# Channel attention: queries and keys projected once, and laid into the score strips through a strip image in DRAM

## What is computed

```python
q = jnp.einsum('oc,bct->bot', Wq, target) + bq[None, :, None]      # target: normalised x, 128 x 256 per batch
k = jnp.einsum('oc,bcs->bos', Wk, source) + bk[None, :, None]      # source: context
v = jnp.einsum('oc,bcs->bos', Wv, source) + bv[None, :, None]
# 16 heads of 8 rows each
dot = jnp.einsum('bhdt,bhds->bhts', q, k) / math.sqrt(HEAD_DIM)
mask = target_mask[:, :, :, None] * source_mask[:, :, None, :]
dot = mask * dot - (1.0 - mask) * NEG
amap = jax.nn.softmax(dot, axis=-1) * mask
out = jnp.einsum('bhts,bhds->bhdt', amap, v)
```

## Time and profile before

| | |
|---|---|
| median of 3 runs | 1764.23 us (1762.54 to 1769.84) |
| profiled execution | 1761.46 us, span of its trace 1759.6 us |
| mean granted clock | 0.984 |
| busy, share of the span | PE 95%, DVE 65%, ACT 56%, POOL 33% |
| channel attention | until about 310 us |
| a batch of it in the middle | 15.05 us |

### The profile page before, as it was taken

One profiled execution on the slowest core, in us unless ns is written; L12 is line 12 of the kernel. 1 busy time (PEld: TensorE's weight loads), 2 busy tenths in 40 slices (PEclk: granted clock), 3 DMA queues, 4 the chain that ended last, 5 costly groups with the idle time before them and its releaser, 6 DMA issues. The chain is left out here.

```text
span 1759.6 us, 34328 instructions
## 1 busy us (share of the span) xinstructions
PE 1676.9 (95%) x11824; PEld 1419.5 (81%) x11832; DVE 1139.4 (65%) x2540; ACT 992.1 (56%) x2502; POOL 584.2 (33%) x638
## 2 busy tenths in 40 slices
PE   7999997798999999999999999999999998899997
PEld 6666664368788988889898989888898997689985
DVE  6888888897556656656566655555555567954434
ACT  2788875686545555545556555545545543555553
POOL 4444426435511111112122111111111212877774
PEclk9999997899999999999999999999999999999999
DMA  6011122102100100100100011001000004443448
GB/s 209 14 31 32 32 81 96 60 1 101 52 13 13 45 5 14 49 1 13 37 25 25 13 65 37 13 1 37 13 1 13 1 1 122 146 120 118 127 114 291
DMA packets 50371, 95.95 MB, mean 55 GB/s; under 512 B 10838, under 2 KB 30598, under 8 KB 49216
## 3 DMA queue, kind: packets, MB, share of 16 engines
q1 hardware_dynamic: 41619, 71.09, 12.8%
q0 software_dynamic: 7584, 21.37, 4.1%
q10 hardware_dynamic: 1000, 1.26, 0.2%
HBM read 73.85 MB, written 19.25 MB: 53 GB/s over the span
## 5 line engine op out<-in xcount | busy, mean ns | idle before, releaser
L2358 POOL TENSOR_TENSOR hold_wq<-hold_wq,ca_rsum 128x512 f32<-128x512 f32 x128 | 133.9, 1046 | 797.9 <-DVE ca_rsum L2600 797.9
L2218 ACT ACTIVATE hold_wq<-ca_pT 128x512 f32<-128x512 f32 x128 | 76.4, 597 | 381.3 <-PE ca_pT L2425 381.3
L1116 DVE TENSOR_REDUCE a_mx<-a_s 128x2 f32<-128x512 f32 x256 | 164.1, 684 | 37.5 <-PE a_s L959 37.1
L2581 DVE COPY ca_values<-ca_v 128x512 f32<-128x512 f32 x128 | 88.4, 690 | 125.0 <-PE ca_v L2377 124.3
L2375 PE MATMUL ca_qk<-early_x,cw_wqkv_h 128*128 128x512 f32 x384 | 161.0, 419 | 1.3 <-PEq L1577 1.3
L2590 DVE TENSOR_TENSOR hold_wq<-ca_s,hold_wk 128x512 f32<-128x512 f32 x128 | 88.3, 690 | 108.1 <-PE ca_s L2418 105.2
L845 ACT ACTIVATE a_prob<-a_s 128x512 f32<-128x512 f32 x256 | 138.1, 594 | 34.3 <-PE a_s L979 30.8
L2377 PE MATMUL ca_qk<-early_x,cw_wqkv_l 128*128 128x512 f32 x384 | 151.7, 395 | 0.0
L2376 PE MATMUL ca_qk<-early_x,cw_wqkv_h 128*128 128x512 f32 x384 | 151.2, 394 | 0.0
L2498 PE MATMUL ca_acc<-ca_wo_h,ca_oT_l 128*128 128x256 f32 x512 | 145.2, 284 | 0.0
L2497 PE MATMUL ca_acc<-ca_wo_l,ca_oT_h 128*128 128x256 f32 x512 | 145.0, 283 | 0.0
(11 more groups left out here) (540 smaller groups left out, 4667.2 us busy)
## 6 DMA issues: line engine op xcount, KB each, us to landing
early_big<-slot_results SPq DMA_DIRECT2D x16, 512.0 KB, 7.1
mw_raw<-in_d_expert_w SPq DMA_DIRECT2D x12, 352.0 KB, 5.1
mw_down<-in_d_expert_d SPq DMA_DIRECT2D x1, 2816.0 KB
a_wraw<-a_heads SPq DMA_DIRECT2D x17, 128.0 KB, 2.0
token_rows<-early_rows SPq DMA_DIRECT2D x1, 2176.0 KB, 15.3
hold_wk<-in_c_wkT SPq DMA_DIRECT2D x1, 2064.0 KB
hold_wq<-in_c_wqT SPq DMA_DIRECT2D x1, 2064.0 KB, 8.2
a_heads<-a_osb SPq DMA_DIRECT2D x64, 32.0 KB
```

Of the source, the lines that this page charges most:

```text
L1116: dve.tensor_reduce(mx[:, b % 2, :, h], s1_bank(b, u)[:, :, :], AX.X, ALU.max)\
L2358: pool.tensor_tensor(prob[:, k % 2, :, :], prob[:, k % 2, :, :], rsum[:, k % 2, :].unsqueeze(2).broadcast_to([P, GB, TOKENS]), ALU.mult)\
```

## The change

From batch 3 on (`WHOLE_ROWS`) q and k are projected once: `whn`, `wln` and `bextn` are the weights and biases in natural order, 128 columns each for q and k, copied out of the strips by POOL. One `join` per batch takes the place of the four pieces: both q and k in one bank, two bias products and six products of parts, in slot 8 of batch b - 2 (`JOIN`), for batch 3 in slot 32; the pieces stood in slots 0, 4, 8 and 12 of batch b - 1. ACT rounds the bank once (`round_pair`), DVE takes the rest once (`rest_pair`). SP then sends the high parts (twice each) and the rests (once each) into a strip image in DRAM, `a_strips`, six transfers of [128 x 256] (`send_parts`), and when these have landed reads the image into `qs` and `ks`, two transfers of [128 x 1024] (`load_strips`). The mask rows and zero rows of the image are written once: POOL makes the mask rows for all batches (`mask_rows`), SP sends them (`send_masks`, eight transfers of 13 batches x 16 heads x 256) and the zeros (`send_zeros`, two of 3 batches before the loop, two of 10 batches in the round of batch 1). The value products of these batches move from slots 13 and 15 to slots 5 and 13. POOL makes all four parts of a batch together at slot 0. `close` moves two slots back. Batches 0 to 2 are made as before.

```diff
+        strips = nc.dram_tensor("a_strips", (2, BATCHES, A_ROWS, P // A_HD * DIM), F32, kind="Internal").ap()
...
-        CLOSING, INVERTED = 35, 9
+        CLOSING, INVERTED = 37, 11
...
+        JOIN, VALUES, MASKED, ZEROED = 8, (5, 13), 4, 6
...
+                def send_masks():
+                    sp.wait_ge(mrow_ready, 8)
+                    later = slice(WHOLE_ROWS, BATCHES)
+                    for k in range(2):
+                        for i in range(4):
+                            sp.dma_start(strips[k, later, 24 + i, :].rearrange("b (h n) -> b h n", n=DIM),
+                                         mrow[k][later, i, :].bitcast(F32).unsqueeze(1)
+                                         .broadcast_to([BATCHES - WHOLE_ROWS, A_HEADS, DIM])).then_inc(mrow_sent, 16)
+
+                def send_zeros(a, b):
+                    for k in range(2):
+                        sp.dma_start(strips[k, a:b, 28:32, :].rearrange("b i (h n) -> b (i h) n", n=DIM),
+                                     mext[a:b, 0:DIM].bitcast(F32).unsqueeze(1).broadcast_to([b - a, 4 * A_HEADS, DIM]))\
+                          .then_inc(zeros_sent, 16)
+
+                def send_parts(b):
+                    p, n = b % 2, b - WHOLE_ROWS + 1
+                    sp.wait_ge(qk_hi, n)
+                    for k, c in ((0, 0), (0, 1), (1, 0), (1, 2)):
+                        sp.dma_start(strips[k, b, 8 * c:8 * c + 8, :].rearrange("d (h n) -> (d h) n", n=DIM),
+                                     hi[:, p, k, :].bitcast(F32)).then_inc(hi_sent[p], 16)
+                    sp.wait_ge(qk_lo, n)
+                    for k, c in ((0, 2), (1, 1)):
+                        sp.dma_start(strips[k, b, 8 * c:8 * c + 8, :].rearrange("d (h n) -> (d h) n", n=DIM),
+                                     low[:, p, k, :].bitcast(F32)).then_inc(lo_sent[p], 16)
+
+                def load_strips(b):
+                    p, i = b % 2, (b - WHOLE_ROWS) // 2
...
+                    sp.wait_ge(hi_sent[p], 64 * (i + 1))
+                    sp.wait_ge(lo_sent[p], 32 * (i + 1))
+                    after(sp, s2_psum, U * (b - A_BUFS + 1))
+                    for k, t in enumerate((qs, ks)):
+                        sp.dma_start(t[:, b % A_BUFS, :, :].rearrange("p j n -> p (j n)").bitcast(F32),
+                                     strips[k, b].rearrange("p (r j) -> r p j", r=A_SLOTS)).then_inc(strip_in[p], 16)
+
                 maxima(0)
+                send_masks()
+                send_zeros(WHOLE_ROWS, ZEROED)
                 maxima(1)
+                send_parts(WHOLE_ROWS)
+                load_strips(WHOLE_ROWS)
                 for b in range(BATCHES):
+                    if b == 1:
+                        send_zeros(ZEROED, BATCHES)
+                    if b + 4 < BATCHES:
+                        send_parts(b + 4)
...
                     gather(b)
                     if b + 2 < BATCHES:
                         maxima(b + 2)
+                    if b + 4 < BATCHES:
+                        load_strips(b + 4)
...
+                def join(b):
+                    pe.wait_ge(xl_ready, b + 1)
+                    pe.wait_ge(cl_ready, b + 1)
+                    for k, (h, l) in enumerate(((xh, xl), (ch, cl))):
+                        o = proj[0][:, k, :]
+                        pe.matmul(o, whn[:, k, :], h[:, b % 2, :], start=False, stop=False, skip_group_check=True)
+                        pe.matmul(o, whn[:, k, :], l[:, b % 2, :], start=False, stop=False, skip_group_check=True)
+                        mm = pe.matmul(o, wln[:, k, :], h[:, b % 2, :], start=False, stop=True, skip_group_check=True)
+                    mm.then_inc(qk_psum, 1)
...
+                        if u == 0 and b >= WHOLE_ROWS:
+                            pe.wait_ge(strip_in[b % 2], 32 * ((b - WHOLE_ROWS) // 2 + 1))
```

More of the change, by code:

```diff
@@ L490, in built, with pieces, joined, value_half @@
             return t // U + 1 if t // U + 1 < BATCHES else None
+        def pieces(t):
+            b = built(t)
+            return b if b is not None and b < WHOLE_ROWS else None
+        def joined(t):
+            b = WHOLE_ROWS if t == U * (WHOLE_ROWS - 1) else (t - JOIN) // U + 2 if (t - JOIN) % U == 0 else -1
+            return b if WHOLE_ROWS <= b < BATCHES and (b > WHOLE_ROWS or t == U * (WHOLE_ROWS - 1)) else None
+        def value_half(t):
+            b, u = built(t), t % U
+            if b is None or u not in (VALUES if b >= WHOLE_ROWS else (13, 15)):
+                return None
+            return b, (VALUES if b >= WHOLE_ROWS else (13, 15)).index(u)
+        def values_read(t):
+            if 0 <= t < ALL and t % U == 0 and t // U < WHOLE_ROWS:
+                return t // U
+            return built(t) if built(t) is not None and built(t) >= WHOLE_ROWS and t % U == VALUES[1] + 1 else None
         def turned(t):
@@ L562, in freed @@
             if k < 0:
+                return
+            if b >= WHOLE_ROWS:
+                if kind == "v":
+                    eng.wait_ge(k_stack, 2 * WHOLE_ROWS)
+                    eng.wait_ge(v_ready, b)
+                else:
+                    eng.wait_ge(v_ready, WHOLE_ROWS)
+                    after(eng, qk_lo, b - WHOLE_ROWS)
                 return
@@ L860, in before_exponentials @@
                         read_maxima(turned(t - 1))
[L861 to L864 removed]
+                    if pieces(t) is not None and u in (2, 6, 10, 14):
+                        round_piece(pieces(t), *PIECES[u - 2])
+                    if joined(t - 2) is not None:
+                        round_pair(joined(t - 2))
+                    if values_read(t) is not None:
+                        read_v(values_read(t))
                     if copied(t) is not None:
@@ L1022, in products @@
                 def products(t):
-                    u, b = t % U, built(t)
                     if weighed(t):
                         weigh(*weighed(t))
-                    if b is not None:
-                        if u in (0, 4, 8, 12):
-                            project(b, *PIECES[u], 0)
-                            project(b, *PIECES[u], 1)
-                        if u in (13, 15):
-                            project_v(b, (u - 13) // 2)
+                    if pieces(t) is not None and t % U in PIECES:
+                        project(pieces(t), *PIECES[t % U], 0)
+                        project(pieces(t), *PIECES[t % U], 1)
+                    if joined(t) is not None:
+                        join(joined(t))
+                    if value_half(t):
+                        project_v(*value_half(t))
                     if turned(t) is not None:
@@ L1054, in _ @@
                     for t in both:
-                        if built(t) is not None and built(t) >= WHOLE_ROWS and t % U in PIECES:
-                            bias(built(t), *PIECES[t % U])
+                        if joined(t) is not None:
+                            join_bias(joined(t))
+                        if value_half(t) and value_half(t)[0] >= WHOLE_ROWS and value_half(t)[1] == 0:
+                            bias_v(value_half(t)[0])
                     for t in both:
@@ L1147, in _ @@
                             take_max(*unit1(n))
-                    u, b = t % U, built(t)
-                    if b is not None and u in (2, 6, 10, 14):
-                        stack_piece(b, *PIECES[u - 2])
+                    if pieces(t) is not None and t % U in (2, 6, 10, 14):
+                        stack_piece(pieces(t), *PIECES[t % U - 2])
+                    if joined(t - 2) is not None:
+                        rest_pair(joined(t - 2))
                     if FIRST <= t - MEASURED + FIRST < BATCHES:
```

115 lines of the change are left out of this document (85 added, 30 removed).

## The result

| | before | after |
|---|---|---|
| median | 1764.0 us (1762.5 to 1769.8) | 1904.4 us (1902.6 to 1906.5) |
| ratio | | 1.079, 95% interval 1.076 to 1.082 |
| span of the profiled execution | 1759.6 | 1900.8 |
| mean granted clock | 0.984 | 0.918 |
| last exponential begins | 300.5 | 442.5 |

The change makes the kernel 140 us slower. The prediction had the direction and the mechanism, but 75 us, and its range ended at 1885.

What follows compares the result with a forecast made beforehand. PE looked like the bound before; after the change SP's serial round of 19.6 us would set the batch. Added 6.7 + 2.0 + 16.1 + 41 + 9.5 = 75 us over 1761.5 gave 1836, range 1800 to 1885.

Steps and rivals of the forecast that it cites:

- PE and ACT's own floor of 13.4: Channel attention: eight pairs of exponentials at 1.67 us, 13.4 us a batch if nothing new were late.
- The ordinary batch: SP's serial round in steady channel attention: 19.6 us against 15.05 before, nine batches adding 41 us.
- The loads to the landing of the inverses: Step of SP's round: 1.2 us to first data, 10.2 loading on four engines, 0.1 landing; 11.5 us.
- The parts: Step of SP's round: four issues at 0.38 us and two more behind the rest, 2.4 us.
- Mask rows: SP's 1.7 MB behind the first maxima, from 13 neighbouring partitions: 6.3 to 16.7 us, middle 11.5 taken.
- Start and second batch: Late strips of batch 3 add 6.7 us at slot 48; the next batch, queued behind those loads, adds 2.0.
- Zero rows in round 1: SP's 1.3 MB on ten engines ahead of everything in batch 1's round: 11.5 plus the ordinary 4.6, 16.1 us.
- The fetch batch: Round of batch 11, with 2 MB of weights ahead: 4.9 plus the ordinary 4.6, 9.5 us added.
- Clock: PE's stops halve its clock, mostly hidden under the round; 0 to 2 us a batch, up to +24, upper range only.
- Sixteen engines: Rival: strip loads spread over sixteen engines, batch of 13.4 us, kernel 1750 or 1742 us; chance 0.08.
- slow reads: Rival: strip loads run below the weights' rate, reading 4 KB pieces 16 KB apart; 1950 to past 2000 us; chance 0.05.
- Only the four engines bind: Rival: transfers overlap SP's waits, first four engines set 16.2 us a batch, kernel 1800 us; chance 0.06.

Runs made afterwards that it cites:

- e9: Changed kernel with mask rows copied within DRAM, no zero rows sent, inverses before loads, four 28-row loads, merged high-part sends: 1751.1 us, 0.990 of the kernel before.
- e2: Changed kernel with each 128-row strip load cut into four loads of 32 rows, one per strip: 1826.2 us.
- e1: Changed kernel with the inverses stored and spread ahead of the two strip loads on SyncE: 1869.4 us.
- e4: Changed kernel with the ten batches' zero rows read from SBUF rows 12 partitions apart instead of neighbouring rows: 1881.3 us.
- e5: Changed kernel with the zero rows written from 64 rows of a tile of zeros, those 64 rows outermost: 1881.2 us.
- e10: Changed kernel with unused products, ten ahead of PE's wait for the strips and four ahead of its wait for the maxima: 1908.1 us.
- e3: Changed kernel with the two strip loads issued by ScalarE on its own queue instead of by SyncE: 1869.4 us.
- e12: e9 with four unused products ahead of PE's wait for the strips of each batch: 1757.9 us, 0.995 of the kernel before.

## Why the prediction was off

*Direction, place and mechanism: right.* Loads on four engines, the inverses behind them, PE stopping at both waits of a batch, PE and ACT's own floor of 13.4 (13.5 in e9), nothing given back behind the stage. e2 shows the engine count, e1 and e2 the serial wait. What failed is sizes, and one step that was left out.

*The ordinary batch: 19.6 forecast, 23.15 measured, which is 31 of the 65 us.* Two terms were small. The loads to the landing of the inverses were put at 11.5 and are 13.6 to 13.7 to the next issue. By the trace's records of packets, in the round of 170.44, the data take 11.5 us from first to last and not 10.2: 1.05 MB at 91 GB/s over the whole, the lower end named in the prediction (the maxima), where the rate of the large transfer was taken. To it come 1.3 us from the load's issue to its first data, about as forecast, and 0.75 from its last packet to the issue of the spread, where 0.1 was put. The parts were put at 2.4 us and are 3.2 to 3.9: the four sends take 2.04 to 2.84 instead of 1.53, and the two behind take 0.95 to 1.5. The other links, 4.5 and 0.7, were right.

*Mask rows: 11.5 us forecast, 22 measured, above the upper bound of 16.7.* The price was made per engine, thirteen engines at 8 to 21 GB/s each, and the limit was not there: e4 has the same engines per byte and pays 48 ns for 1 KB where the changed kernel pays 124. A safer bound would have come from the nearest row with few SBUF partitions as a source, as one rate for them together: the heads' 63 GB/s, which gives 27 us for 1.7 MB. The prediction used that row only per engine.

*What the slow mask rows hold up.* The sum followed only batch 3's strips. On SyncE the maxima of batch 1 stood behind the masks, at 71.13, and cost 17.70 us of ACT's time before batch 3 was wanted. This was one queue to be walked through for everything moved behind it, and that step was left out: the sum has no term for those maxima. Start and second batch: 30 us instead of 9. The time of 72.4 at which slot 48 would want its strips does not follow from the pairs that it names, which reach 70.6; nothing in the sum hangs on it.

*Zero rows in round 1: 16.1 forecast, 26.9 measured.* The same mis-sized source (11.5 us put in, some 20 measured: from 118.81 until the parts behind them are out at 142.57, less the parts' own 3.7). In this interval e4 and e5 give 14 and 13 us back; the rest of their 23 comes from the first zero rows. That the sums of batch 1 would be late behind them, and stop DVE and through it PE, was not in the prediction either.

*The fetch batch: 9.5 forecast, 11.3 measured.* The interval takes 27.6, 3.0 above the 24.6 forecast for it: about the ordinary batch's error again. Before the change it took 16.3 and not 15.05.

*Clock: 0 to 2 us a batch in the upper range.* Nothing of it shows (e10, where a part of the clock came back and no time with it), as the central value had it. The argument, that eight pairs at half clock need less than the round, fits that.

*The rivals.* Sixteen engines and slow reads did not occur. "Only the four engines bind" was priced at 16.2; e1 and e3, where they come nearest to it, gave 20.3 and 19.7, since by the rounds above heads, reading back, maxima, inverses and spread pass those engines one after another, each waiting for the last.

*The range.* Its upper end took the bounds of the loads, of masks and zeros and of the clock from rows, and left out the other victims of a full queue. 1904 lies 19 us above it. Open is why the parts' issues take 0.5 us in the steady round and 0.38 for the heads; no run varied that.

## What to carry to other kernels

Read a DMA's cost by three things, and go by the one that allows least: the engines that its slowest dimension gives, the SBUF rows that its source or target reaches (neighbours share), and what stands ahead on the same engines, whichever queue issued it. A transfer put on a serial queue must be walked past everything behind it, small transfers for a different batch too; making this load wide was worth 78 us, reordering it 35, another queue for it 35. The half clock cost nothing that showed under a longer chain, and 4 to 6 us a batch in e9, where that chain is gone.

## What the runs showed of the hardware

- Ten neighbouring SBUF rows as a source gave 74 GB/s with nine engines busy, ten rows 12 partitions apart 238 GB/s (the parts of a batch on the engines left free are in both), 64 neighbouring ones 195.
- Behind large transfers on few engines the issue itself becomes long: four issues took 17.93 us, against 2.04 in the steady round.
- DRAM to DRAM, with the 16 heads outermost, 1 KB pieces at places 512 KB apart moved at 236 GB/s.
- A store of 128 packets behind two loads on four engines moved three quarters of them at once and the last quarter 10 us later; with the loads on ScalarE's queue it took 7.5 us to land, and 1.4 with nothing ahead.
- In e9 three stops of PE, the longest 1.5 us, were followed by a granted clock of 0.50 for some 34 us; in e12, with 1.2 us of unused products in each batch, it stayed at 1.00 from 60 to 220 us.
